# Attention scores with heads in pairs: 64-row matmuls on half the array each, and two-bank operations, in a gated cross-attention and expert layer

## The reference

```
qh = (layernorm(x) @ Wq) -> 16 heads of 64        # x: 512 x 256 per batch
kh, vh = ctx @ Wk, ctx @ Wv -> 16 heads of 64     # ctx: 512 x 128 per batch
attn = softmax(qh @ kh.T * 64**-0.5)
x = x + tanh(g_xattn) * (concat(attn @ vh) @ Wo + bo)
comb = top-2 of softmax(layernorm(x) @ gate_w.T), zero elsewhere
x = x + tanh(g_ffn) * sum_e comb[:, e] * (layernorm(x) @ expert_w[e].T + expert_b[e])
```

## Time and profile before

| | |
|---|---|
| median of 3 runs | 1213.12 us (1210.05 to 1215.27) |
| the profiled execution | 1210.17 us, of which the span is 1208.5 us |
| mean granted TensorE clock | 0.989 of full speed |
| busy share of the span | PE 94%, PEld 76%, DVE 81%, ACT 70%, POOL 54% |
| small row DMAs (QB<-nmax) | 512 of 0.5 KB, median 1.9 us from issue to landing |
| copies QA<-QA and KB<-KA | 64 each, 256 KB, median 3.0 us |

### The profile page before, as it was taken

How to read it: one execution, slowest core, us unless ns; L and a number is a source line. 1 busy time by engine, 2 the same in 40 slices (tenths; PEclk the granted TensorE clock), 3 DMA queues, 4 the chain that set the end, 5 groups by cost and what they waited for, 6 DMA issues and landing times.

```text
span 1208.5 us, 30873 instructions
## 1 busy us (share of the span) xinstructions
PE 1135.7 (94%) x10592; PEld 913.4 (76%) x10592; DVE 979.0 (81%) x1945; ACT 849.6 (70%) x1531; POOL 648.0 (54%) x579
## 2 busy tenths in 40 slices
PE   4888999999999999999899999999999999999968
PEld 3677777788778887788777887778877788778846
DVE  7788878987898778987789877898778887897646
ACT  4888888676876678676786768867687677866610
POOL 2566666455655547455564545645556455654610
PEclk8999999999999999999999999999999999999979
DMA  4333212122221122221222112211122121121000
GB/s 133 78 85 79 37 37 54 29 37 45 37 53 29 28 54 36 46 37 27 57 37 45 28 37 45 54 36 28 41 50 45 28 37 40 33 37 36 2 19 17
DMA packets 97521, 51.79 MB, mean 43 GB/s; under 512 B 77000, under 2 KB 86608, under 8 KB 97360
## 3 DMA queue, kind: packets, MB, share of 16 engines
q1 hardware_dynamic: 97360, 49.74, 20.3%
HBM read 11.68 MB, written 4.19 MB: 13 GB/s over the span
## 4 chain that ended last, share of the span: by engine, by line
PE 70%; DVE 15%; issue 7%; DMA 3%; ACT 3%; SPq 1%; DVEq 0%; POOL 0%; ACTq 0%
PE MB L934 30%; PE PV L1057 12%; PE MX L1037 8%; PE ST L1047 7%; PE ST L1044 7%; DVE nmax L767 3%; DVE KA L744 3%; PE MB L944 3%; DMA QB<-nmax 2%; DVE QB L739 1%; PE MB L1014 1%; DVE stats L656 1%; DVE w L879 1%; SPq L432 1%; DVE m L886 1%
## 5 line engine op out<-in xcount | busy, mean ns | idle before, releaser
L514 POOL TENSOR_TENSOR p_s<-pf,p_s 128x512 f16<-128x512 f32 x512 | 594.7, 1169 | 496.1 <-ACT p_s L621 492.5
L596 ACT ACTIVATE pf<-ST 128x512 f32<-128x512 f32 x512 | 306.2, 599 | 193.0 <-PE ST L1047 186.3
L767 DVE TENSOR_REDUCE nmax<-MX 128x1 fp32r<-128x512 f32 x512 | 347.2, 685 | 69.0 <-PE MX L1037 60.9
L621 ACT ACTIVATE p_s<-pf 128x512 f16<-128x512 f32 x512 | 318.1, 629 | 45.1 <-PE PV L1057 42.0
L1037 PE MATMUL MX<-KA,QA 128*128 128x512 f32 x512 | 216.9, 426 | 18.6 <-DVE nmax L767 15.2
L1057 PEld LDWEIGHTS PV<-v_s,p_s 128*128 128x128 f16 x6144 | 193.6, 98 | 33.6 <-issue 24.7
L1047 PE MATMUL ST<-QB,KB 65*128 65x512 f32 x512 | 204.8, 400 | 7.2 <-DMA QB<-nmax 7.0
L1057 PE MATMUL PV<-v_s,p_s 128*128 128x65 f16 x6144 | 209.0, 194 | 1.3 <-POOL p_s L514 1.3
L1044 PE MATMUL ST<-QA,KA 128*128 128x512 f32 x512 | 206.2, 403 | 3.6 <-ACT pf L596 3.1
L934 PE MATMUL MB<-ex_s,x2t_s 128*128 128x512 f32 x708 | 188.8, 402 | 3.2 <-DVE KA L744 3.2
L934 PEld LDWEIGHTS MB<-ex_s,x2t_s 128*128 128x128 f32 x708 | 128.1, 188 | 34.9 <-DVE KA L744 6.3
(11 more groups left out here) (120 smaller groups left out, 1113.4 us busy)
## 6 DMA issues: line engine op xcount, KB each, us to landing
QA<-QA SPq DMA_DIRECT2D x64, 256.0 KB, 3.0
KB<-KA SPq DMA_DIRECT2D x64, 256.0 KB, 3.0
QB<-nmax SPq DMA_DIRECT2D x512, 0.5 KB, 1.9
xin<-x SPq DMA_DIRECT2D x8, 512.0 KB, 4.0
out<-acc SPq DMA_DIRECT2D x8, 512.0 KB, 3.2
kvin<-kv_t SPq DMA_DIRECT2D x8, 256.0 KB, 4.2
acc<-expert_t SPq DMA_DIRECT2D x8, 256.0 KB, 3.3
acc<-wo SPq DMA_DIRECT2D x4, 256.0 KB, 3.3
```

Of the source, the lines that this page charges most:

```text
L514: pool.tensor_tensor(p_s[:, h % 2, 1, t, :], pf[:, t, :], p_s[:, h % 2, 0, t, :], ALU.subtract)\
L596: act.activation(pf[:, t, :], st_bank(h, t)[:, :], ACT.Exp, bias=P_SHIFT, scale=SCALE)\
L621: act.activation(p_s[:, h % 2, 0, t, :], pf[:, t, :], ACT.Copy).then_inc(p_hi, 1)
L767: dve.tensor_reduce(nmax[:, h % 2, t:t + 1], MX[t % 2][:, :], AX.X, ALU.max, negate=True)\
```

## The change

A head pair stays in 128 partitions as the projection leaves it. `QH`, `QL`, `KH`, `KL` hold high and low parts with the first head in rows 0 to 63 and the second in rows 64 to 127, so ACT and DVE take a q or k job in one operation, and the DMA copies `QA<-QA` and `KB<-KA` are gone. Work goes by units, one query tile of a pair: 32 units per turn instead of 64 tiles. A unit's scores are four terms (high keys by high queries, low by high, high by low, and `KX` by `QX` for the maxima, where row 0 and row 64 of `KX` are ones and all other rows are zeros). Each term is two 64-row matmuls, rows 0 to 63 for the first head into one bank of ST, rows 64 to 127 for the second into the other; in the built program they are placed on the upper and on the lower half of the array. The maxima are two 64-row matmuls (high by high) into two banks of MX. The reduction, the exponential, the f16 copy and POOL's subtraction handle both banks at once (1024 columns). The number of row DMAs is the same. MX and ST are now one buffer of two banks each, where they were two buffers of one bank; `pf` has two buffers of a unit. The maxima run five units ahead (`AHEAD`). The tables are written anew: a unit's scores and maxima stand together, and values and jobs stand between them.

```diff
-    (10, 0): [("expert", 1, 1)], (10, 1): [("q", 7)], (10, 2): [("wo", 1, 0)], (10, 3): [("k", 7)],
+    (10, 1): [("q", 7), ("k", 7)], (10, 2): [("wo", 1, 0)],
...
-PE_ORDER = (
-    ('scores maximum values jobs',
-     'maximum scores jobs values',
...
+AHEAD = 5
+VALUES_AT = ((0, 3), (1, 1))
+NORMALISE_AT = ((1, 0), (1, 2))
+PE_ORDER = (('scores maximum jobs', 'values jobs', 'scores maximum jobs', 'values jobs'), ('scores maximum jobs', 'values jobs', 'scores maximum jobs', 'values jobs'))
...
-                if kind in ("q", "k"):
-                    dst, s = (QA if kind == "q" else KA), it.pair_slot(name)
-                    act.activation(dst[0:HEAD, s, :], m[0:HEAD, :], ACT.Copy)
-                    last = act.activation(dst[0:HEAD, s + 1, :], m[HEAD:P, :], ACT.Copy)
+                    last = act.activation((QH if kind == "q" else KH)[:, it.pair_slot(name), :], m[:, :], ACT.Copy)
...
-                        act.activation(pf[:, t, :], st_bank(h, t)[:, :], ACT.Exp, bias=P_SHIFT, scale=SCALE)\
+                        act.activation(pf[:, u % 2, :, :], ST[:, :, :], ACT.Exp, bias=P_SHIFT, scale=SCALE)\
...
-                dve.tensor_reduce(nmax[:, h % 2, t:t + 1], MX[t % 2][:, :], AX.X, ALU.max, negate=True)\
+                dve.tensor_reduce(nmax[:, p % 2, t, :], MX[:, :, :], AX.X, ALU.max, negate=True).then_inc(max_free, 1)
...
-                pe.matmul(st_bank(h, t)[:, :], KA[:, s, tile(t)], QA[:, s, :], start=True, stop=False)
-                if t == 0:
-                    pe.wait_ge(row_in[h % 2], row_count(b, h))
-                pe.matmul(st_bank(h, t)[:, :], KB[0:HEAD + 1, s, tile(t)], QB[0:HEAD + 1, s, :],
-                          start=False, stop=True).then_inc(st_ready, 1)
+                for i in range(2):
+                    r = pair_rows(i)
+                    last = pe.matmul(MX[:, i, :], QH[r, s, tile(t)], KH[r, s, :], start=True, stop=True)
+                last.then_inc(max_ready, 1)
+
+            def scores(it, p, t):
+
+                b, s = it.b, it.slot(p)
+                pe.wait_ge(st_free, unit_count(b, p, t))
+                terms = ((KH[:, s, tile(t)], QH[:, s, :]), (KL[:, s, tile(t)], QH[:, s, :]),
+                         (KH[:, s, tile(t)], QL[:, s, :]), (KX[:, :], QX[:, s, :]))
+                for n, (keys, queries) in enumerate(terms):
+                    if (t, n) == (0, len(terms) - 1):
+                        pe.wait_ge(row_in[p % 2], row_count(b, p))
+                    for i in range(2):
+                        r = pair_rows(i)
+                        last = pe.matmul(ST[:, i, :], keys[r, :], queries[r, :], start=(n == 0),
+                                         stop=(n == len(terms) - 1))
+                last.then_inc(st_ready, 1)
```

More of the change, by code:

```diff
@@ L121 @@
+LN2_AT = (3, 0)
+LN2_APPLY_AT = (3, 3)
 LN2_POWER_AT = (3, 0)
@@ L182, in __init__, with slot, keys_done @@
         self.kind, self.b, self.turn = kind, b, turn
-    def head_slot(self, h):
-        return 2 * ((PAIRS * self.turn + h // 2) % SLOTS) + h % 2
+    def slot(self, p):
+        return (PAIRS * self.turn + p) % SLOTS
     def pair_slot(self, name):
-        ahead = PAIRS if self.kind != PRO and name in NEXT_JOBS else 0
-        return self.head_slot(2 * (name[1] + ahead))
+        return self.slot(name[1] + (PAIRS if self.kind != PRO and name in NEXT_JOBS else 0))
+    def keys_done(self, lists, p):
+        if self.kind == PRO or p >= 2:
+            return self.done(lists, ("k", p % PAIRS))
+        return self.done_before(lists, ("k", p))
     def start(self, lists):
@@ L251, in bank, with banks @@
             return ctx.enter_context(nc.psum_tensor(name, [P, 512], F32))
+        def banks(name):
+            return ctx.enter_context(nc.psum_tensor(name, [P, 2, 512], F32))
         def sem(name):
@@ L417, in _, with row @@
             sp.dma_start(gt_f[:, :, :], gate_t.rearrange("(c p) e -> p c e", p=P)).then_inc(small_in, 16)
[L419 to L434, removed]
-            pro = Iteration(PRO, 0, 0)
[L437 to L443, removed]
+            def row(it, p, t):
+                sp.wait_ge(max_free, unit_count(it.b, p, t) + 1)
+                for i in range(2):
+                    sp.dma_start(QX[HEAD * i:HEAD * i + 1, it.slot(p), t * P:(t + 1) * P].bitcast(F32),
+                                 nmax[:, p % 2, t, i:i + 1].bitcast(F32), allow_slow_non_contiguous=True)\
+                      .then_inc(row_in[p % 2], 16)
+            pro = Iteration(PRO, 0, 0)
+            sp.wait_ge(const_pool, CONST_POOL + 4)
+            for u in range(AHEAD):
+                row(pro, *divmod(u, TT))
             def before(it):
@@ L806, in _ @@
                 take(pro, name)
-            for t in range(TT // 2):
-                maximum(0, 1, t)
+            for u in range(TT, AHEAD):
+                maximum(0, *divmod(u, TT))
             def outputs_scale(b):
@@ L821, in slot @@
                     if part == "normalise":
-                        if t == NORMALISE_SLOT and (h >= VALUES_BACK or kind != FIRST):
-                            if h == VALUES_BACK:
+                        if (h % 2, t) in NORMALISE_AT and (h >= 2 or kind != FIRST):
+                            head = h // 2 * 2 - 2 + NORMALISE_AT.index((h % 2, t))
+                            if head == 0:
                                 outputs_scale(b)
-                            normalise(b, h - VALUES_BACK)
+                            normalise(b, head)
                     elif part == "whole":
@@ L1077, in _ @@
                 produce(pro, name)
-            for t in range(TT // 2):
-                maximum(pro, 1, t)
-            pe.wait_ge(const_dve, 1)
+            pe.wait_ge(job_hi, pro.keys_done(HI, 1))
+            for u in range(TT, AHEAD):
+                maximum(pro, *divmod(u, TT))
+            pe.wait_ge(const_pool, CONST_POOL + 4)
             def slot(it, h, t):
                 b, kind = it.b, it.kind
-                p, ahead = h // 2, (h + 2) // 2 % PAIRS
-                if h % 2 == 0 and t == 0:
-                    pe.wait_ge(k_dup[p % 2], dup_count(b, p))
+                p, u = unit_of(h, t)
```

226 lines of the change are left out of this document (98 added, 128 removed), and 12 rows, old and new, of the table PLACED.

## The result

The changed kernel takes 1221.29 us (median of 9 runs, 1217.45 to 1225.87) against 1215.27 us before (9 runs, 1210.05 to 1218.86): ratio 1.0055, 95% interval 1.0032 to 1.0079. It is slower by 0.5%; the forecast was 2.0%. Its profiled execution took 1217.45 us, 7.3 us more than that of before, at a mean granted clock of 0.990 against 0.989, so the clock is no part of that difference.

What follows compares the result with a forecast made beforehand. PE's pace through its list was taken as the bound. 1210.2 - 60.2 + 97.3 + 26.9 - 40 = 1234.2 us, plus 3 us to the median of the runs: 1237 us, 2.0% slower; range of 8 in 10: 1150 to 1310.

Steps and rivals of the forecast that it cites:

- Fewer passes: Scores and maxima on PE: paired 64-row matmuls overlap fully, five passes a unit instead of six, 60.2 us gained.
- Changes of rows: Around each unit's block on PE: a round trip between 128-row and 64-row matmuls costs 0.38 us, 97.3 us in all.
- the prediction's own sign, a round trip under 0.25 us: Test on PE's row changes: the prediction is wrong if a round trip between 64 and 128 rows costs under 0.25 us.
- The second head's lag: At a block's start on PE: the second head's weight load starts 0.105 us behind the first's, costing 26.9 us.
- the Trainium skill's rule: Matmuls on different row groups start about 4 ns apart, loads overlapped: no lag; cited under the cheap round trip, chance 0.33.
- Waits of PE: PE's waits for `nmax`, row DMA and keys all go, 37 us, plus 3 us in the prologue: 40 us gained.
- A term that was put at nothing: At a block's start on PE: the exposed weight load was counted as new, inside the 0.38 us round trip.
- DVE near 850 us: DVE's work falls from 979 to 850 us: 41 us less in reductions, 88 us less in q and k low parts.

Runs made afterwards that it cites:

- e1: Changed kernel with every score and maxima term as one 128-row matmul, both heads summed, so no change of rows (part of the result left out); 1160.0 us.
- e5: Changed kernel with an extra one-column 128-row matmul between a unit's scores and maxima, outside the prologue, adding one round trip between 64 and 128 rows; 1331.65 us.
- e6: Changed kernel with an extra one-column 64-row matmul between a unit's scores and maxima, outside the prologue, adding no change of rows; 1261.84 us.
- e2: Changed kernel with all four score terms of the first head listed ahead of the four of the second, same matmuls; 1222.32 us.
- e3: Changed kernel with POOL's subtraction as two operations of 512 columns instead of one of 1024; 1217.5 us.

## Why the prediction came out as it did

The direction and the mechanism held, and the size did not: +24 us on the profiled pair was forecast, +7.3 measured. By the prediction's own terms:

- *Fewer passes*, -60.2 us. Right: full overlap. Passes of a block stand 0.233 us apart where 0.235 was taken, which makes it -63 (six passes of 0.235 against five of 0.233, 256 times).
- *Changes of rows*, +97.3 us. Right in size: at a block that stands between full 512-column matmuls a round trip is 0.38 to 0.39 us. Where transposes follow a block the last step is some 0.06 instead of 0.10, and where `PV` follows, 0.01. Summed over all units it is 94 us in place. Taken away (e1) it gives back 61; added once more (e5 less e6) it costs 70. So the prediction's own sign, a round trip under 0.25 us, is not met in place and is just met by what e1 gives back.
- *The second head's lag*, +26.9 us. **This step failed.** It took the 0.10 us between two full loads for halves as well. The loads of the two halves start 3 ns apart. The lag is nothing, and this alone is 27 us of the miss. The bounds held it (0 to 0.105); the choice of the end went by rows in which two loads share array rows, and the Trainium skill's rule (TensorE: Matmul & The Clock Gate, The mechanism), cited in the prediction as a rival, was the better one.
- *Waits of PE*, -40 us. **This step failed too**, the other way. Of the earlier trace rows the row DMA (7.0) and the key (6.4) went as forecast, and the first keys' 3.0 with them; `nmax` stayed (15.2, now 15.6), and in the room of the others came `v_s` (7.5), `PV`'s wait for `o_n` (5.7) and small ones: idle is 58.3 and 58.7 us. Counted from the pace (0.165 us a wait, 36 fewer waits) that is -6. e1 and e5 show why a wait comes back: PE's idle depends on how early PE arrives. The idle is 70.8 us where the kernel is 61 us shorter, and 40.8 where e5 makes it 110 longer.
- *A term that was put at nothing.* The prediction counts the exposed load at the start of a block as new. The kernel before paid some of it already, without a change of rows: a 512-column matmul of scores or maxima right behind short matmuls is followed after 0.31 to 0.32 us instead of 0.233, in 128 places, 11 us in all; and a matmul that PE had waited for is followed late as well, 8.5 us in all, of which 1.4 are left. In the changed kernel both lie inside the steps that are counted above. That is -18. The kernel before, behind the values and behind full matmuls:

```profile
600.71 1.64 PE L1057 MATMUL PV<-v_s,p_s 128*128 128x65 f16 x48
602.18 0.47 PE L1037 MATMUL MX<-KA,QA 128*128 128x512 f32 x1
602.49 0.39 PE L1044 MATMUL ST<-QA,KA 128*128 128x512 f32 x1
602.72 0.39 PE L1047 MATMUL ST<-QB,KB 65*128 65x512 f32 x1
```

- *DVE near 850 us.* Measured 883.9. In the durations of the operations the low parts fell by 88 us as priced and the reductions by 39 (41 forecast), and small operations held up by POOL (last section) gained some 9. The rest, 23 us, is a matter of the count: the records of successive operations overlap a little, so busy time is 70 us below the sum of the durations before and 47 after, with 385 fewer operations.

Together: -63 + 94 + 0 - 6 - 18 = +7. The forecast was 17 us high: by 3 us at the passes, 3 at the changes of rows, 27 at the lag and 18 at the term that it left out, less 34 that it booked for waits and did not get. That these errors nearly cancel is luck. The sizes of the terms are worked out from the starts of PE's matmuls in one execution of each kernel, and each is good to a few microseconds.

What is not settled: what q and k taken whole would bring in the tables of before, which was not tried; and whether other tables would let the changed kernel keep more of it (three tries gave 4 us at most).

## What to carry to other kernels

Two 64-row matmuls on different halves of the array run as one pass, loads included, and need no alternation in the list; but each passage between 64-row and 128-row work costs 0.09 us before the first matmul and up to 0.10 of exposed load behind it. So long blocks should pay better than short ones, which no run here tried (here a block of five passes saved one, 0.23 us, and paid 0.38 in place, 0.24 when it was taken away). Behind short matmuls 0.08 of that load is exposed in any case, so a passage costs less there. Count passages per unit before counting passes. And don't book a wait of PE as won because its releaser gets faster: ask what stands next in line there, and how much earlier PE will arrive.

## What the runs showed of the hardware

- Between half-array matmuls PE did not keep the order of the list (e2): four terms of one head stood before the other's first, and they ran in pairs.
- Small operations of DVE stand while POOL subtracts. The group with the largest loss, after (count | busy us, mean ns | idle before):

```profile
L866 DVE TENSOR_TENSOR prob<-prob,r 128x32 f32<-128x32 f32 x8 | 12.0, 1498 | 0.3
```

Before:

```profile
L896 DVE TENSOR_TENSOR prob<-prob,r 128x32 f32<-128x32 f32 x8 | 1.5, 192 | 0.3
```

The longest single `m<-w,r` (the same shape) took 1182 ns before, with POOL's operation at 1169, and 2033 after, with it at 2150; in e3 1111. After, 28 of the 104 operations of this shape last over 400 ns, and all 28 end within 0.06 us of the end of an operation of POOL (before 29, all 29). The reductions from PSUM do not show it (1219 ns by the earlier trace rows's 1210). The Trainium skill (SBUF — State Buffer, Who interferes with whom) has a rule that a DVE operation with two SBUF inputs and a GpSimd operation that reads SBUF exclude each other for the whole instruction; by that, the traces agree. A longer operation on POOL makes the hold longer.
